# ScalarE issues the repeated loads of four edge stages of a graph network kernel

## The reference

```python
# layer 0: convolution
msg = silu(h[src] + (edge_attr @ we.T + be)); agg = segment_sum(msg, dst)
x = layernorm(x + graph_norm(silu((1 + eps) * h + agg) + x))
# layer 1: attention with one softmax over all edges
e = leaky_relu(h[row] @ a_src + h[col] @ a_dst + a_b); att = softmax(e, axis=0)
x = layernorm(x + segment_sum(att * h[col], row))
# layer 2: 8 heads, softmax per target node
score = clip(einsum(K[src], Q[dst]) / 4, -5, 5); ...; x = layernorm(x + segment_sum(V[src] * a, dst))
# layer 3: relation MLP on (x[src], x[dst], edge_attr), summed at the target, then an MLP per node
x = layernorm(x + update(x, segment_sum(mlp([x[src], x[dst], edge_attr]), dst)))
```

## Time and profile before

| | us |
|---|---|
| median of 3 runs | 6209.27 (6199.66 to 6213.69) |
| span of the profiled execution | 6321.6 |
| PE, PEld, DVE, ACT, POOL busy in it | 4256.0, 3740.8, 2983.7, 1666.9, 3424.5 |
| its DMA traffic | 645.54 MB, mean 102 GB/s |

### The profile page before, as it was taken

The page is one execution under the profiler, slowest core; times in us unless marked ns, Lnnn a source line. Parts: engine busy times, 40 slices in busy tenths (PEclk is TensorE's granted clock), DMA queues, the critical chain, the costliest instruction groups (busy, mean ns, idle before and its releaser), DMA issues. The chain is left out here.

```text
span 6321.6 us, 91693 instructions
## 1 busy us (share of the span) xinstructions
PE 4256.0 (67%) x19917; PEld 3740.8 (59%) x19918; DVE 2983.7 (47%) x8050; ACT 1666.9 (26%) x2996; POOL 3424.5 (54%) x3536
## 2 busy tenths in 40 slices
PE   3555555556777777787855555555568888888887
PEld 3444544445766777776744445445456666667765
DVE  5444444456332333235755555555564444444445
ACT  0111111113222222226732222222233333333331
POOL 3655655532566656566635556555525555555550
PEclk6666566666555555558976666666679999998999
DMA  4233323234222222225733333333334444444441
GB/s 103 81 83 83 83 78 82 80 71 109 78 80 80 80 80 81 79 77 169 206 99 99 100 97 101 99 101 97 98 105 131 132 131 133 128 128 132 133 128 48
DMA packets 491156, 645.54 MB, mean 102 GB/s; under 512 B 94519, under 2 KB 354059, under 8 KB 490798
## 3 DMA queue, kind: packets, MB, share of 16 engines
q0 software_dynamic: 132032, 325.99, 18.1%
q1 hardware_dynamic: 346462, 312.02, 17.6%
q10 hardware_dynamic: 12560, 6.52, 0.6%
HBM read 554.38 MB, written 89.82 MB: 102 GB/s over the span
## 5 line engine op out<-in xcount | busy, mean ns | idle before, releaser
L1610 POOL DMA_INDIRECT R<-table_ps,r_idx x832 | 809.6, 973 | 731.9 <-DVE r_idx L1684 417.5
L1195 POOL DMA_INDIRECT by_src<-R,p_idx x832 | 826.3, 993 | 627.9 <-issue 246.0
L1390 POOL DMA_INDIRECT R<-table_kv,h_idx x832 | 805.3, 968 | 647.7 <-issue 324.3
L660 POOL DMA_INDIRECT R<-table,c_idx x784 | 750.5, 957 | 548.5 <-issue 307.7
L1420 PE MATMUL psum<-R,h_oh 128*128 128x137 f32 x1664 | 405.0, 415 | 627.8 <-issue 291.4
L693 PE MATMUL psum<-R,c_oh 128*128 x1664 | 380.1, 400 | 620.4 <-DVE R L752 375.0
L1420 PEld LDWEIGHTS psum<-R,h_oh 128*128 128x128 f32 x1664 | 344.2, 295 | 679.8 <-issue 494.5
L693 PEld LDWEIGHTS psum<-R,c_oh 128*128 128x128 f32 x1664 | 324.3, 290 | 673.5 <-issue 673.5
L1632 PE MATMUL psum<-w_L_gnn_re_w,r_ea 128*128 128x256 f32 x1664 | 555.3, 417 | 226.5 <-DVE X L1724 209.7
L1745 DVE TENSOR_TENSOR R<-R,psum 128x256 f32 x832 | 346.9, 417 | 752.0 <-remote 344.6
L1008 PE MATMUL psum<-R 128*128 x1664 | 428.5, 424 | 189.0 <-issue 187.0
(11 more groups left out here) (339 smaller groups left out, 7696.9 us busy)
## 6 DMA issues: line engine op xcount, KB each, us to landing
R<-by_src SPq DMA_DIRECT2D x220, 260.0 KB, 3.1
r_ea<-in_ea_t SPq DMA_DIRECT2D x832, 64.0 KB
R<-in_ea_t SPq DMA_DIRECT2D x196, 256.0 KB
R<-rel_rows SPq DMA_DIRECT2D x104, 256.0 KB
R<-lo_rows SPq DMA_DIRECT2D x104, 256.0 KB
h_rel<-rel_rows SPq DMA_DIRECT2D x208, 128.0 KB
r_rel<-rel_rows SPq DMA_DIRECT2D x208, 128.0 KB
by_src<-R,p_idx POOLq DMA_INDIRECT x832
```

Of the source, the lines that this page charges most:

```text
L660: g.indirect_dma_start(out=rows[:, u, :], out_offset=None, in_=table, in_offset=bass.IndirectOffsetOnAxis(ap=idx[:, j // GROUPS % 2, u:u + ...
L1195: g.indirect_dma_start(out=by_src, out_offset=bass.IndirectOffsetOnAxis(ap=idx[:, u:u + 1], axis=0), in_=rows[:, u, :], in_offset=None).th ...
L1390: g.indirect_dma_start(out=rows[:, u, :], out_offset=None, in_=table, in_offset=bass.IndirectOffsetOnAxis(ap=idx[:, u:u + 1], axis=0)).the ...
L1610: g.indirect_dma_start(out=rows[:, u, :], out_offset=None, in_=table, in_offset=bass.IndirectOffsetOnAxis(ap=idx[:, u:u + 1], axis=0)).the ...
```

## The change

SP now issues only the first load of each buffer. All later ones are issued by ACT as a function of its pipeline, at a turn where its own waits already say that the buffer is free, or behind one more wait. The semaphores `ea_free` and `sp_turn` go, and with `ea_free` PE's wait for its own products. `pipeline` gets `ahead`, which takes that many turns out of the loop at the end, where there is nothing left to load.

```diff
 # pipeline
-    rounds = (iters * per - begin) // per
+    rounds = (iters * per - begin - ahead) // per
 # convolution, SP
-                def load(i, j):
-                    sp.wait_ge(ea_free, PER * i + j + 1)
-                    sp.dma_start(ea[:, j % GROUPS, :], ...).then_inc(ea_in[j % GROUPS], 16)
-                staggered(sp, PER, (load, 0, TILE_GROUPS))
+                for j in range(GROUPS):
+                    sp.dma_start(ea[:, j, :], ...).then_inc(ea_in[j], 16)
 # convolution, PE, end of edge_product
-                    pe.wait_ge(product, n + 1)
-                    pe.sem_inc(ea_free, 1)
 # convolution, ACT
+                def load_ahead(i, j):
+                    a.dma_start(ea[:, j % GROUPS, :], k.ea_t[:, bass.ds((PER * i + j + GROUPS) * (G * P), G * P)]
+                                ).then_inc(ea_in[j % GROUPS], 16)
-                staggered(a, PER, (act, 0, TILE_GROUPS))
+                staggered(a, PER, (act, 0, TILE_GROUPS), (load_ahead, 0, TILE_GROUPS - GROUPS))
 # placing, ACT (SP's loop over rel, lo and digits goes)
+                def next_lo(i, j):          # dma_start only
+                def next_rel(i, j):
+                        a.wait_ge(rel_used, PER * i + j + 1 + PER)
+                        a.dma_start(rel[:, j, :], ...).then_inc(rel_in[j], 16)
+                def next_digits(i, j):
+                        a.wait_ge(placed_done, PER * i + j + 1 + PER)
+                        a.dma_start(digits[0:3, j, :], ...).then_inc(digit_in[j], 16)
-                pipeline(a, ITERS, PER, distance, is_nought, copy, lags=(0, 0, 1), loads=PER + 1)
+                pipeline(a, ITERS, PER, distance, is_nought, next_lo, next_digits, next_rel, copy, lags=(0, 0, 0, 1, 1, 1),
+                         loads=PER + 1, ahead=PER)
 # heads, ACT (SP's loop over rel goes)
-                pipeline(a, ITERS, GROUPS, distance, is_nought, weigh, lags=(0, 1, 3), loads=4)
+                pipeline(a, ITERS, GROUPS, distance, is_nought, load_ahead, weigh, lags=(0, 1, 1, 3), loads=4, ahead=GROUPS)
 # relation, ACT (SP's loop over rel and ea goes)
+                def next_ea(i, j):
+                        if j == 0:
+                            regs["tile"] = load_steps(nc, a, k.ek[0], (i + 1) * U, ET - 1)
+                        for u in range(G * j, G * j + G):
+                            a.dma_start(ea[:, u, :], k.ea_t[:, bass.ds(regs["tile"][u] * P, P)]).then_inc(ea_in[u], 16)
-                pipeline(a, ITERS, GROUPS, distance, is_nought, act, lags=(0, 1, 3), loads=4)
+                pipeline(a, ITERS, GROUPS, distance, is_nought, next_rel, act, next_ea, lags=(0, 1, 1, 3, 3), loads=3, ahead=GROUPS)
```

## The result

The changed kernel takes 6284.36 us (median of 6 runs, 6263.85 to 6298.38), the kernel before 6217.64 beside it (6 runs, 6199.66 to 6243.86): 1.0098 of before, 95% interval 1.0073 to 1.0122, or +61 us (+45 to +76). Forecast were 6195 us and a gain of 14. The profiled execution of the changed kernel took 6294.25 us with a span of 6292.4.

The account below looks back on a forecast made before the run. No engine fills a stage; rings of hand-overs, partly late, bound them, and SP's issue is off the path. Convolution -17 and relation +3 make -14 us, from 6209.3 to 6195 us (-0.22%); range 6150 to 6250.

Parts of the forecast that it names:

- Convolution, -17: Convolution: without PE's wait for its own products the sums start on time; 17 us less, bounds nothing to 23.6.
- lateness of the sums behind the register read: Convolution: PE's 1.107 us read of ring slots delays the sums every fourth group; 23.6 us in all, 0.71 of it gained.
- together 52: Convolution: late waits of the sums, 41 ended by "issue" at 0.33 us and 11 by ACT at 0.92 us.
- Placing, 0: Placing: three issues and landing take 4.7 to 5.8 us, inside 6.9; cost 0, or 52 us if half the groups fell short.
- Heads, 0: Heads: one ACT issue a group hides under `is_nought`'s 0.72 us activation; cost 0, as ACT waits 385 us there.
- upper bound of 104 us: Heads: the cost if the issues of 208 groups, 0.5 us each, were laid end to end.
- Relation, +3: Relation: five loads a group on ACT, free in plain turns; 3 us as the value, 20 us at the most.
- 3.0 us of slack behind `is_nought`: Relation: in a turn without pause `is_nought` ends 3.0 us before PE's weight load for it, so plain turns cost 0.
- The slow rival: Relation: ACT's four issues take 3.7 to 5.1 us in half the groups; 48 us likely, less 17: 6240; chance 0.20.
- does not involve the loads: All four stages: part of each is hand-over arriving late while POOL issues, which the loads have no part in.
- one rival in which they shrink: Heads and placing: fewer semaphores and a silent SP shorten late hand-overs by 88 us, giving 6104; chance 0.05.
- a change of over 20 us in such stages: Sign of being wrong: stages with late hand-overs change by more than 20 us; right meant others within 5 us each.

Follow-up runs that it names:

- again: The kernel before, unchanged, profiled a second time on a late chip, where hand-overs between engines come late: 6213.59 us, span 6211.8.
- all_b: The whole change against the kernel before, on a prompt chip, where late hand-overs are nearly all missing: ratio 0.9977 (0.9968 to 0.9987).

## Why the prediction was wrong

- **Convolution, -17: the size was right in part by luck.** Alone it gave -17 us (-31 to -4). The lateness of the sums behind the register read is real and goes, and TensorE's sequencer does read ahead. But some 13 us of it go where 23.6 were priced, and of the "together 52" turns only 31 to 39 are late; times 0.71 that is 9 us. And a gain of -15 stays when the wait stays, so the wait is not its whole reason: the raise behind it and the load's later time were given no part of their own. The rule of the Trainium skill, "DMA: Bandwidth & Descriptors", section "Issuing engines are not separate DMA queues", that another issuer saves only the sequencer's time, would have given 0 for the move. It holds in so far as the issuer made no difference (-17 with ScalarE, -11 with SP, intervals overlapping); what it leaves out is that the load also moved in time.
- **Placing, 0: right**, -5 us (-21 to +12).
- **Heads, 0: the step that failed.** "ACT waits 385 us there, so 0" took a sum of waits for slack. They are waits of `is_nought`, ahead of the issue, and the instruction behind it, `weigh`, was left out. On prompt chips the cost is indeed nothing. On late chips the stage grows by some 55 us, and `weigh`'s late hand-overs go from 18 to 52; messages, sums and POOL's next gathers stand behind a late `weigh`. Some 40 of the 55 us by the gathers, some 30 by the totals, go when the issue doesn't stand ahead of `weigh`. This is most of the miss. The upper bound of 104 us held, but it was left out of the forecast and given no rival.
- **Relation, +3: too small by a factor of ten.** The usual price (1.88 us for four, 1.84 in the median) was right, and so was the slack on DVE's add. What failed is the 3.0 us of slack behind `is_nought`, read from one turn and taken for all, and the late groups, which were to pass it "by up to 1 us": 14 groups take over 4.1 us and up to 8.0. Measured +29 (+13 to +46), by the gathers from `ea` ahead of `distance`. (The hold of 2.3 us every fourth group is also a slip: 0.9 and 1.1 are 2.0.)
- **The slow rival** had the sign and, with 6240, about half of the loss. Its condition, over 4.1 us for a group's issues, comes true in relation in 14 to 22 of 204 groups, not in half of them, and its price there before the 17 us of gain, 48 us, is at the upper end of the +29 (+13 to +46). Its sign, PE waiting for `is_nought` by name, did not come. It was laid in relation only; heads' single issue was thought too short to matter.
- **The late hand-overs** were taken as "does not involve the loads", with one rival in which they shrink. Those of `weigh` grew, from 120.1 to 335.6 us, those of `is_nought` did not. The prediction named a change of over 20 us in such stages as the sign of being wrong, and that is what came. Why an issue just ahead of `weigh` makes them more frequent stays open; twice the number of issues, and twice their time, made it no worse.
- **The base.** Stage lengths were taken from a trace 112 us above the runs. The median was used for the time, so this cost no accuracy in the total, but the first trace alone would have shown heads 1382 us long before and 1391 after, and hidden the loss.

## What to carry to other kernels

Price a DMA issue put into a computing engine's queue by the instruction that stands behind it, and not by its 0.34 us alone: in these runs it cost little ahead of an instruction that waits long anyway (relation's `ea` behind `is_nought` cost nothing that shows, ahead of `distance` some 30 us), and much ahead of one for which the next engines wait (heads' `weigh`). When the traces show hand-overs of 5 us without a cause, waits beside them are no slack to spend; and before an edit of under 1% is judged by stages, the unchanged kernel is to be profiled a second time. A gain of the right size does not prove its reason. A run that keeps the suspected wait tells only if it keeps all that goes with it, here the raise too, and if its interval is narrower than what it asks for; the start of one instruction behind the end of another, read over all turns of two traces, told a few us where the totals could not.

## What the runs showed of the hardware

- The same kernel takes 6219, 6224 and 6220 us on three chips and 5155 and 5153 on two. The gathers take the same there (median 946 to 949 ns in heads), and POOL's work too, within 2%. What differs most is hand-overs that come up to 17 us late in the stages with gathers and scatters. The granted clock differs as well (heads 0.66 in `again`, 0.75 in `all_b`); whether it follows from the longer pauses was not tested. The worst of the late hand-overs on DVE are the first two rows, from the unchanged kernel on a late chip. The third is the same wait as the first (L1745, here L1746) with heads alone changed on a prompt chip, where it names its releaser:

```profile
DVE R L1745 <- remote: 475.3, 79, 8.5
DVE R L1141 <- remote: 472.8, 45, 16.6
```
```profile
DVE R L1746 <- PE psum L1645: 379.2, 207, 4.0
```
- The sign of an edit can depend on this: the whole change is +1.0% on one kind of chip and -0.2% on the other.
- On late chips DMA issues can be slow on ScalarE as on SP: four of them took 1.84 us in the median and up to 8.0 (14 groups of 204 over 4.1 us), on a prompt chip never over 2.7.
- PE's queue reads registers ahead of its own matmuls: without the wait in between, the 1.107 us read of ring slots started, in the turn shown, 1.3 us before the products that stand ahead of it in the program. A wait and a raise between them put it 0.30 us behind their end, the wait alone 0.15.
